# First attention: normalising and rounding on ScalarE, a ninth summand that centres the sums, one bias product for two v tiles

## Chip, cores, metric

One core of a Trainium2 chip (trn2). The metric is the device time of one execution in microseconds (us); of several runs the median is taken.

## The reference

Two blocks of attention and mixture of experts over 4 x 1024 tokens of 256 numbers, all in float32. The change touches only the first attention, which has no softmax: every token mixes its own heads.

```python
xn = _layernorm(x)
q = (xn @ Wq.T + bq)      # 16 heads of 16;  k, v: 8 heads of 16, each used by two heads of q
q = q * cos + _rotate_half(q) * sin          # k the same
def _softmax_kernel(x, R):                   # R: 8 x 16
    n = jnp.sqrt(jnp.sum(x * x, axis=-1, keepdims=True))
    x = x / jnp.maximum(n, 1e-06)
    p = jnp.einsum('...d,ed->...e', x, R)
    return jnp.concatenate([jnp.sin(p), jnp.cos(p)], axis=-1) / math.sqrt(F)
kv = jnp.einsum('bhsf,bhsd->bsfd', kp, v)    # sum over heads, position by position
out = jnp.einsum('bhsf,bsfd->bhsd', qp, kv)
g = _silu(_L0_ffn_ref(xn, L0_ffn_wg, ...))   # 8 experts, the two best of each token
x = x + (out @ Wo.T + bo) * g
```

The product of a q head's features with a k head's is a sum of cosines of eight angle differences. The kernel computes it as the sum of sin^2(pi * d) over the eight differences d (in turns), less 4, with the factor -2 folded into other constants. The second block (causal attention, 16 experts, a shared expert) follows.

## The kernel before

The kernel runs phase by phase with a barrier between. The first is `first_attention`. It goes over 32 tiles of 128 tokens in software-pipelined steps. `in_steps(eng, (lag, stage), ...)` writes each engine's program: in step n it calls every stage with tile n - lag, in the order of its list, after `beside(n)`, which holds work with a pace of its own in the first 24 steps (`BESIDE`). Within an engine the order is that of the program; between engines semaphores connect them. A tile passes through these stages (engine, lag):

- Ahead of the steps ScalarE makes the high half of the weights (`w_all[0]`). A product in float32 is made as three passes of high and low halves (`three_passes`, whose matmuls all stand under L121).
- `statistics` (VectorE, `beside`, four tiles in each of steps 0 to 7) gives mean and variance, `root` (ScalarE, at the start of `beside` of the same step) the square root, `inverse_root` (VectorE, one step later) its inverse. `normalise` (VectorE, L519) writes a pair of normalised tiles to `rows`, one pair in step 1 and two in each step after.
- `transpose` (TensorE) transposes one pair a step, `high_half` (ScalarE) copies it out of PSUM, `low_half` (VectorE, one step later) writes the rest.
- `project` (TensorE, 2): q and k of one tile, seven matmuls, the last with the bias: two rows of ones by `b_two`, which holds the high and low half of all biases. `values_and_logits`: v and the routing logits of a pair, at the end of the step, seven matmuls for each tile, each with its own bias matmul (L778).
- `take_qkv` (ScalarE, 2) copies q and k out (`qk`) and writes their squares (`sq`); `rotate` (GpSimd, 2) makes the rotary step; `square_norm` (VectorE, 3, L530) sums the squares; `transpose_rotated` (TensorE, 3), `keep_rotT` (ScalarE, 3), `random_projection` (TensorE, 4), `keep_p` (ScalarE, 4).
- `norm` (ScalarE, 4), `bounded_norm` and `inverse_norm` (VectorE, 5) work on four tiles at a time, in every fourth step. The root and the sine need different ScalarE tables, so each such step has two table loads.
- `in_turns` (VectorE, 8, L551) gives p divided by the norm and by 2 pi; `whole_turns` (L556) rounds it by adding and subtracting a large constant `ROUND`; `fraction` (L562) is the difference. `differences` (VectorE, 9, L570) writes all q minus k angles to `apart` (16 x 8 x 8 per token), `sines` and `squares` (ScalarE, 10), `sine_sums` (VectorE, 11, L576) sums eight of them to `A`, `centre` (L580) subtracts 4, `weigh` (VectorE, 11, L589) multiplies with v, 2048 numbers per token: the large product.
- `sum_groups` (TensorE, 12, L803) sums the eight groups in PSUM, `take_out` (ScalarE, 13), `store` (SyncE, 14).

In steps 18 to 23 VectorE also does the routing of the experts, which needs all logits. From its step 24 on GpSimd scatters the normalised rows to the experts' slots by indirect DMA, beside the rotations. VectorE's step before is, in this order:

```python
in_steps(dve, (5, bounded_norm), (11, sine_sums), (5, inverse_norm), (8, in_turns), (11, centre), (8, whole_turns), (11, weigh),
         (8, fraction), (3, square_norm), (9, differences), first=BESIDE, beside=beside)
```

## Time and profile before

| | |
|---|---|
| Median of 3 runs | 1822.14 us (1820.26 to 1829.56) |
| Profiled execution | 1824.24 us, span 1822.5 us |
| TensorE, VectorE, ScalarE, GpSimd busy | 1599.4, 1377.4, 1031.1, 669.7 us |
| First attention | the first 322 us of the span |

An execution's own time is a little above the span, which runs from the first to the last recorded instruction. Busy times count overlapping instructions once. An engine that is busy need not be the bound: a VectorE instruction also counts as busy while something outside the program's waits holds it up.

### The profile page before, as it was taken

Reading aid. Unit: us, or ns where it says so; the run is one execution under the profiler, and the core shown is the slowest. Engines: PE = TensorE matmul, PEld = TensorE weight load, DVE = VectorE, ACT = ScalarE, POOL = GpSimd, SP = SyncE. Lnnn points to the kernel's source line nnn. Section 1 sums busy time; section 2 is a strip of 40 time slices with the busy share of each in tenths; the row PEclk is TensorE's granted clock in tenths of the full one; section 3 lists DMA queues with packets and bytes.
Section 4 is the critical chain, followed back from the end, with each engine's and each line's share of the span. In section 5 each row is a group of like instructions: output and inputs, shape, how many; then the busy total and the mean of one; then the engine's idle time right before and its main releaser. Section 6 shows DMA issues by size and latency. Waiting matters only on the chain. (4 is left out here: it accounts for less than half of the span.)

```text
span 1822.5 us, 34561 instructions
## 1 busy us (share of the span) xinstructions
PE 1599.4 (88%) x9650; PEld 1239.4 (68%) x9650; DVE 1377.4 (76%) x3710; ACT 1031.1 (57%) x2457; POOL 669.7 (37%) x842
## 2 busy tenths in 40 slices
PE   5997887889936777999999999987899999998896
PEld 4885666689934564554555555544799999877775
DVE  6899999366667869999888888823666666667777
ACT  2664564356646750665676767674566666543443
POOL 2655688400047613212247676610000000066662
PEclk8998899989976995999999999998999999999998
DMA  9433457744436885322436454424864444355552
GB/s 345 131 87 95 105 133 174 247 132 133 131 114 195 289 318 133 68 64 70 108 95 176 139 165 151 131 58 147 270 190 134 134 132 133 113 171 162 173 165 74
DMA packets 279591, 272.72 MB, mean 150 GB/s; under 512 B 121769, under 2 KB 248426, under 8 KB 277356
## 3 DMA queue, kind: packets, MB, share of 16 engines
q1 hardware_dynamic: 255672, 215.41, 40.2%
q0 software_dynamic: 18432, 50.36, 9.1%
q10 hardware_dynamic: 5332, 4.96, 0.8%
q8 instruction: 88, 1.44, 0.3%
q14 instruction: 67, 0.55, 0.1%
HBM read 136.84 MB, written 133.69 MB: 148 GB/s over the span
## 5 line engine op out<-in xcount | busy, mean ns | idle before, releaser
L1940 ACT ACTIVATE ca_PT<-ca_psS 128x512 f32<-128x512 f32 (+3 forms) x768 | 336.4, 494 | 203.5 <-PE ca_psS L1977 198.6
L1480 POOL DMA_INDIRECT g_y<-ys_scratch,pos x128 | 125.1, 977 | 427.1 <-POOLq L73 356.0
L1856 DVE CUSTOM_DVE_ANT_0 ca_masked_row<-ca_psM,mask_row 128x384 f32<-128x384 f32 (+3 forms) x512 | 224.2, 486 | 44.8 <-PE ca_psM L1960 42.8
L1977 PE MATMUL ca_psS<-ca_QS,ca_KS 128*128 128x512 f32 (+1 forms) x480 | 175.3, 369 | 1.4 <-ACT ca_PT L1940 1.4
L1860 DVE TENSOR_REDUCE ca_part<-ca_psM 128x1 f32<-128x512 f32 x256 | 163.5, 684 | 16.9 <-PE ca_psM L1960 15.6
L1989 PE MATMUL ca_psO<-ca_PT,ca_VA 128*17 128x512 f32 (+3 forms) x1536 | 161.6, 493 | 6.1 <-ACT ca_OT L1932 6.1
L1960 PE MATMUL ca_psM<-ca_KS,ca_QS 126*128 126x512 f32 (+2 forms) x480 | 159.8, 381 | 5.0 <-DVE ca_part L1856 3.8
L803 PE MATMUL fa_psO<-fa_weighed,ident 128*128 128x256 f32 x512 | 130.9, 414 | 37.0 <-DVE fa_weighed L589 36.9
L1977 PEld LDWEIGHTS ca_psS<-ca_QS,ca_KS 128*128 128x128 f32 x480 | 90.6, 190 | 87.6 <-ACT ca_PT L1940 58.5
L391 POOL DMA_INDIRECT xs_scratch<-x_sb,pos x128 | 124.6, 973 | 55.9 <-ACT ca_PT L1940 34.2
L803 PEld LDWEIGHTS fa_psO<-fa_weighed,ident 128*128 128x128 f32 x512 | 103.9, 208 | 58.5 <-DVE fa_weighed L589 43.2
L1032 PE MATMUL f_psU<-ffn_lo,f_x_hi 128*128 x428 | 138.5, 324 | 0.0
L1132 DVE TENSOR_TENSOR f_x_lo<-f_psT,f_x_hi 128x256 fp32r<-128x256 f32 x214 | 90.7, 424 | 49.9 <-ACT f_x_hi L1073 49.7
L1079 ACT ACTIVATE f_silu<-f_psU 128x176 f32<-128x176 f32 x214 | 67.9, 318 | 100.0 <-PE f_psU L1032 99.9
L1831 POOL TENSOR_TENSOR ca_waited<-ca_waited 1x1 f32<-1x1 f32 x128 | 25.6, 200 | 259.3 <-ACT ca_PT L1940 258.0
L1053 PE MATMUL f_psY<-ffn_lo,f_h_hi 128*128 x428 | 120.4, 281 | 0.0
L1960 PE MATMUL ca_psM<-spare 126*128 126x512 f32 (+3 forms) x288 | 98.8, 408 | 16.5 <-DMA ca_VA<-v_scratch 15.9
L1960 PEld LDWEIGHTS ca_psM<-ca_KS,ca_QS 126*128 126x128 f32 x480 | 89.5, 198 | 33.7 <-DVE ca_part L1856 16.5
L1140 DVE TENSOR_TENSOR f_h<-f_silu,f_psU 128x96 f32<-128x96 f32 x214 | 54.2, 253 | 76.8 <-ACT f_silu L1079 76.6
L1977 PE MATMUL ca_psS<-spare 128*128 128x512 f32 (+3 forms) x288 | 104.3, 376 | 2.7 <-ACT ca_PT L1940 2.6
L1032 PE MATMUL f_psU<-ffn_hi,f_x_hi 128*128 x286 | 104.2, 364 | 0.0
L1053 PE MATMUL f_psY<-ffn_hi,f_h_hi 128*128 x286 | 92.4, 323 | 0.3 <-DVE f_h_hi L1149 0.3
(271 smaller groups left out, 4620.6 us busy)
## 6 DMA issues: line engine op xcount, KB each, us to landing
xs_scratch<-fa_blank SPq DMA_DIRECT2D x32, 640.0 KB, 4.9
x_sb<-xs_scratch SPq DMA_DIRECT2D x143, 128.0 KB, 2.1
ys_scratch<-x_sb SPq DMA_DIRECT2D x143, 128.0 KB, 1.7
xs_scratch<-fa_blank SPq DMA_DIRECT2D x32, 384.0 KB, 6.6
spare<-qk_scratch SPq DMA_DIRECT2D x24, 512.0 KB
ca_QS<-qk_scratch SPq DMA_DIRECT2D x20, 512.0 KB
ca_KS<-qk_scratch SPq DMA_DIRECT2D x20, 512.0 KB
x_sb<-in_ffn SPq DMA_DIRECT2D x16, 608.0 KB, 4.1
```

Of the source, the lines that this page charges most:

```text
L391: pool.indirect_dma_start(xs_dram, bass.IndirectOffsetOnAxis(pos[:, t, k:k + 1], 0), rows[:, t, :], None).then_inc(sent[i], 16)
L803: ins = pe.matmul(psO[i % 2][:, 0:NQ], ident[:], weighed[:, i % 2, g, :], start=g == 0, stop=g == KV_HEADS - 1)
L1032: ins = pe.matmul(psU[i % 2][:, 0:WU], x[:, i % 2, k * P:(k + 1) * P], w[:, bass.ds(e, 1), k * WU:(k + 1) * WU].rearrange("p a n -> p (a n)"),
L1053: ins = pe.matmul(psY[i % 2][:, 0:HID], x, w[:, bass.ds(e, 1), first:first + HID].rearrange("p a n -> p (a n)"), start=start, stop=first = ...
L1132: dve.tensor_tensor(x_lo[:, i % 2, :], psT[i % 2][:, 0:HID], x_hi[:, i % 2, :].bitcast(F32), ALU.subtract)\
L1480: pool.indirect_dma_start(y[:, t % R, k, :], None, y_dram, bass.IndirectOffsetOnAxis(pos[:, t, k:k + 1], 0)).then_inc(got[t % R], 16)
L1856: ins = dve.tensor_tensor_reduce(masked_row[:, (n * NU + u) % BANKS, h * w:(h + 1) * w], bank[:, h * w:(h + 1) * w], mask_row[:, CHUNK - w ...
L1860: dve.tensor_reduce(part[:, k0 // CHUNK, h0:h0 + nh, qt], bank[:, 0:nh * w].rearrange("p (h k) -> p h k", h=nh), AX.X, ALU.max).then_inc(u ...
L1940: act.activation(PT[:, s % PTS, h, off:CHUNK], psS[(GH * s + h) % BANKS][:, off:CHUNK], ACT.Exp)\
L1960: ins = pe.matmul(bank[:, h * w:(h + 1) * w], QS[slot][0:STACK, h0 + h, qt * P:(qt + 1) * P], KS[slot][0:STACK, h0 + h, k0:k0 + w], start= ...
L1977: pe.matmul(psS[tile % BANKS][:, off:CHUNK], KS[slot][:, h, kt * P:(kt + 1) * P], QS[slot][:, h, c * CHUNK + off:(c + 1) * CHUNK], start=T ...
L1989: ins = pe.matmul(psO[STRIP * h:STRIP * h + VW, off:CHUNK], VA[:, slot, kt, VW * h:VW * (h + 1)], PT[:, s % PTS, h, off:CHUNK], start=kt = ...
```

## The change

- **Normalising** moves from VectorE to ScalarE: `rows = x * rstd + shift`, with `shift = -mean * rstd` from one more VectorE instruction for each group of four tiles. Pairs 0 and 1 are normalised in step 1, pair n in step n.
- **The root of the variance** moves from the start of ScalarE's step to its end (`after`). A root of one number is put ahead of everything else on ScalarE, so that its table is loaded first.
- **Rounding** (`whole_turns`) moves to ScalarE, between the copy of q and k and their square (`take_qkv` is split in two). `fraction` takes the second half of the rounding along: (whole - ROUND) - turns, which turns the sign of all angles. It now stands behind `square_norm`.
- **Centring**: `apart` gets a ninth column that GpSimd sets to -4 once, the sums read all nine, and `centre` is gone. Differences, sines and squares touch the first eight.
- **Biases of v**: one matmul of 272 columns for both tiles, ahead of their products, in place of one for each tile.
- **Order**: `norm` is the first stage of ScalarE's step. On VectorE the low half of the weights is made ahead of the biases, and `low_half(0)` moves into step 1 between them. `project` waits for the biases only ahead of its first bias matmul.

```diff
@@ first_attention, VectorE
             def inverse_root(g):
-                dve.reciprocal(some, some).then_inc(rstd_done, 1)
-
-            def normalise(q):
-                dve.wait_ge(rstd_done, q * PAIR // GROUP + 1)
-                for t in range(PAIR * q, PAIR * (q + 1)):
-                    dve.tensor_scalar(rows[:, t, :], x_sb[:, t, :], mean_rstd[:, t, 0:1], mean_rstd[:, t, 1:2], ALU.subtract, ALU.mult)\
-                       .then_inc(xn_done, 1)
+                dve.reciprocal(some, some).then_inc(rstd_part, 1)
+                dve.wait_ge(rstd_part, g + 1)
+                dve.scalar_tensor_tensor(shift[:, GROUP * g:GROUP * (g + 1)], mean_rstd[:, GROUP * g:GROUP * (g + 1), 0], -1.0, some,
+                                         ALU.mult, ALU.mult).then_inc(rstd_done, 1)
...
-            def whole_turns(t, i, b):
-                dve.wait_ge(turns_part, t * 2 + 1)
-                dve.tensor_scalar(whole[:, i % 2, :, :], turns[:, i % 2, :, :], ROUND, ROUND, ALU.add, ALU.subtract)\
-                   .then_inc(turns_part, 1)
             def fraction(t, i, b):
-                dve.wait_ge(turns_part, t * 2 + 2)
+                dve.wait_ge(whole_done, t + 1)
                 f = turns[:, i % 2, :, :]
-                dve.tensor_tensor(f, f, whole[:, i % 2, :, :], ALU.subtract).then_inc(turns_done, 1)
+                dve.scalar_tensor_tensor(f, whole[:, i % 2, :, :], ROUND, f, ALU.subtract, ALU.subtract).then_inc(turns_done, 1)
...
-                dve.tensor_tensor(apart[:, i % 2, :, :, :], q4, k4, ALU.subtract).then_inc(apart_done, 1)
+                dve.tensor_tensor(apart[:, i % 2, :, :, 0:RF], q4, k4, ALU.subtract).then_inc(apart_done, 1)
...
-            def centre(t, i, b):
-                dve.wait_ge(A_done, t + 1)
-                dve.tensor_scalar(A[:, i % 2, :, :], A[:, i % 2, :, :], RF / 2.0, None, ALU.subtract).then_inc(centred, 1)
...
-            in_steps(dve, (5, bounded_norm), (11, sine_sums), (5, inverse_norm), (8, in_turns), (11, centre), (8, whole_turns), (11, weigh),
-                     (8, fraction), (3, square_norm), (9, differences), first=BESIDE, beside=beside)
+            in_steps(dve, (5, bounded_norm), (11, sine_sums), (5, inverse_norm), (8, in_turns), (11, weigh), (3, square_norm),
+                     (8, fraction), (9, differences), first=BESIDE, beside=beside)
@@ ScalarE
+            def normalise(q):
+                act.wait_ge(rstd_done, q * PAIR // GROUP + 1)
+                for t in range(PAIR * q, PAIR * (q + 1)):
+                    act.activation(rows[:, t, :], x_sb[:, t, :], ACT.Identity, scale=mean_rstd[:, t, 1:2], bias=shift[:, t:t + 1])\
+                       .then_inc(xn_done, 1)
...
+            def whole_turns(t, i, b):
+                act.wait_ge(turns_part, t + 1)
+                act.activation(whole[:, i % 2, :, :], turns[:, i % 2, :, :], ACT.Copy, bias=ROUND).then_inc(whole_done, 1)
...
             def beside(n):
-                if n < QUADS:
-                    root(n)
+                if n == 1:
+                    normalise(0)
+                    normalise(1)
                 if 0 <= n - 1 < PAIRS:
                     high_half(n - 1)
+                if 2 <= n < PAIRS:
+                    normalise(n)
...
+            def after(n):
+                if n < QUADS:
+                    root(n)
...
-            in_steps(act, (2, take_qkv), (10, sines), (3, keep_rotT), (13, take_out), (10, squares), (4, keep_p),
-                     (4, norm), first=BESIDE, beside=beside)
+            in_steps(act, (4, norm), (2, take_qk), (8, whole_turns), (2, square_qk), (10, sines), (3, keep_rotT), (13, take_out),
+                     (10, squares), (4, keep_p), first=BESIDE, beside=beside, after=after)
@@ TensorE, values_and_logits
+                pe.matmul(psV[:, 0:PAIR * NVE].rearrange("p (t n) -> p t n", n=NVE), ones[:],
+                          b_two[:, NQK:W0].unsqueeze(1).broadcast_to([2, PAIR, NVE]), start=True, stop=False, skip_group_check=True)
                 for j, t in enumerate(range(PAIR * q, PAIR * (q + 1))):
-                    ins = pe.matmul(out, ones[:], b_two[:, NQK:W0], start=False, stop=True, skip_group_check=True)
```

VectorE, a step from the sums on, before (the fa_ names are the first attention's tiles; fa_n are the squared norms, fa_A the sums):

```order
L576 TENSOR_REDUCE fa_A<-fa_apart 128x128
L551 SCALAR_TENSOR_TENSOR fa_turns<-fa_p_sb,fa_inv 128x192
L580 TENSOR_SCALAR fa_A<-fa_A 128x128
L556 TENSOR_SCALAR fa_whole<-fa_turns 128x192
L589 TENSOR_TENSOR fa_weighed<-fa_A,fa_v 128x2048
L562 TENSOR_TENSOR fa_turns<-fa_turns,fa_whole 128x192
L530 TENSOR_REDUCE fa_n<-fa_sq 128x24
L570 TENSOR_TENSOR fa_apart<-fa_turns 128x1024
```

The same stretch with the change:

```order
L573 TENSOR_REDUCE fa_A<-fa_apart 128x128
L553 SCALAR_TENSOR_TENSOR fa_turns<-fa_p_sb,fa_inv 128x192
L582 TENSOR_TENSOR fa_weighed<-fa_A,fa_v 128x2048
L532 TENSOR_REDUCE fa_n<-fa_sq 128x24
L559 SCALAR_TENSOR_TENSOR fa_turns<-fa_whole,fa_turns 128x192
L567 TENSOR_TENSOR fa_apart<-fa_turns 128x128x8
```

Centring and rounding are gone, and the norm's sum stands between the large product and the fraction.

ScalarE, the start of the program, before (spare and wqkvr_raw are the weights and the transposed rows, mean_rstd the statistics, s the normalised rows):

```order
L706 ACT_TABLE_LOAD
L706 ACTIVATE spare<-wqkvr_raw 128x1040
L630 ACT_TABLE_LOAD
L630 ACTIVATE mean_rstd<-mean_rstd 128x4 x2
L636 ACTIVATE spare<-fa_psT 128x512
L630 ACTIVATE mean_rstd<-mean_rstd 128x4
L636 ACTIVATE spare<-fa_psT 128x512
```

And with the change:

```order
L716 ACT_TABLE_LOAD
L716 ACTIVATE fa_warm<-fa_ones 2x1
L718 ACTIVATE spare<-wqkvr_raw 128x1040
L620 ACTIVATE mean_rstd<-mean_rstd 128x4
L625 ACTIVATE s<-x_sb,fa_shift,mean_rstd 128x256 x4
L632 ACTIVATE spare<-fa_psT 128x512
L620 ACTIVATE mean_rstd<-mean_rstd 128x4
L632 ACTIVATE spare<-fa_psT 128x512
```

The second table load is gone, four normalisations stand ahead of the first copy out of PSUM, and the second root, which stood ahead of that copy, stands behind it.

ScalarE, a step with the norms' root, before (the first two rows still belong to the step ahead):

```order
L672 ACT_TABLE_LOAD
L672 ACTIVATE fa_inv<-fa_n 128x96
L636 ACTIVATE spare<-fa_psT 128x512
L642 ACTIVATE fa_v<-fa_psV 128x256
L643 ACTIVATE logits<-fa_psV 128x2x8
L649 ACTIVATE fa_qk<-fa_psQ 128x384
L652 ACTIVATE fa_sq<-fa_psQ 128x384
L677 ACT_TABLE_LOAD
L677 ACTIVATE fa_apart<-fa_apart 128x1024
```

And with the change:

```order
L675 ACT_TABLE_LOAD
L675 ACTIVATE fa_inv<-fa_n 128x96
L645 ACTIVATE fa_qk<-fa_psQ 128x384
L649 ACTIVATE fa_whole<-fa_turns 128x192
L655 ACTIVATE fa_sq<-fa_psQ 128x384
L680 ACT_TABLE_LOAD
L680 ACTIVATE fa_apart<-fa_apart 128x128x8
L661 ACTIVATE fa_rotT<-fa_psR 128x384
```

The root and its load stand ahead of the copy of q and k, and the rounding stands between that copy and the square.

## Rows read from the trace of the kernel before

**Rows 1.** Windows: stretch, length, busy PE, PEld, DVE, ACT, POOL, PEclk, DMA, GB/s.
```profile
0.00:322.00 322.00, 261.90 (x1316) 218.40 (x1316) 293.23 (x459) 165.74 (x309) 196.75 (x186) 0.93 0.54 153
```

**Rows 2.** Windows, two stretches of 20 us.
```profile
100.00:120.00 20.00, 20.00 (x116) 17.40 (x116) 19.91 (x24) 13.81 (x26) 12.90 (x12) 1.00 0.32 79
240.00:260.00 20.00, 17.78 (x92) 14.98 (x92) 19.91 (x25) 13.65 (x23) 18.26 (x17) 1.00 0.51 141
```

**Rows 3.** Timeline, first 20 us, ScalarE and TensorE: start, length, engine, line, tiles [idle before].
```profile
7.72 1.28 ACT L630 ACT_TABLE_LOAD   x1
...
18.37 1.11 PE L757 MATMUL fa_psT<-ident,s 128*128 128x128 f32 x4 [6.94 <-DVE s L519]
19.14 0.67 PE L121 MATMUL fa_psQ<-spare 128*128 128x384 f32 x1
```

**Rows 4.** Timeline from 28 to 75 us, ScalarE and TensorE.
```profile
28.37 0.21 ACT L630 ACTIVATE mean_rstd<-mean_rstd 128x4 f32<-128x4 f32 x1 [5.58 <-DVE mean_rstd L509]
...
29.55 0.45 PE L121 MATMUL fa_psV<-spare 128*128 128x136 f32 x1 [3.10 <-ACT logits L643]
...
34.06 0.67 PE L121 MATMUL fa_psQ<-spare 128*128 128x384 f32 x1
...
74.76 0.42 PE L121 MATMUL fa_psQ<-spare 128*128 128x384 f32 x1
```

**Rows 5.** Windows, granted clock (PEclk) and matmuls (x) of TensorE.
```profile
30.00:44.00 14.00, 14.00 (x54) 12.23 (x54) 9.65 (x30) 3.83 (x12) 6.31 (x8) 0.50 1.07 371
59.00:76.00 17.00, 17.00 (x114) 14.53 (x113) 12.73 (x24) 10.42 (x24) 11.52 (x14) 1.00 0.25 83
```

**Rows 6.** Timeline of TensorE, one step from its v products on.
```profile
96.31 0.27 PE L121 MATMUL fa_psV<-spare 128*128 128x136 f32 x1
...
96.77 0.33 PE L121 MATMUL fa_psV<-spare 128*128 128x136 f32 x1
...
98.26 0.42 PE L121 MATMUL fa_psQ<-spare 128*128 128x384 f32 x1
...
106.82 0.42 PE L121 MATMUL fa_psQ<-spare 128*128 128x384 f32 x1
```

**Rows 7.** Timeline of VectorE, parts of two steps.
```profile
195.45 1.15 DVE L562 TENSOR_TENSOR fa_turns<-fa_turns,fa_whole 128x192 f32<-128x192 f32 x1
196.52 0.54 DVE L530 TENSOR_REDUCE fa_n<-fa_sq 128x24 f32<-128x384 f32 x1
...
200.86 0.22 DVE L580 TENSOR_SCALAR fa_A<-fa_A 128x128 f32<-128x128 f32 x1
200.99 0.25 DVE L556 TENSOR_SCALAR fa_whole<-fa_turns 128x192 f32<-128x192 f32 x1
201.16 2.29 DVE L589 TENSOR_TENSOR fa_weighed<-fa_A,fa_v 128x2048 f32<-128x2048 f32 x1
203.36 0.35 DVE L562 TENSOR_TENSOR fa_turns<-fa_turns,fa_whole 128x192 f32<-128x192 f32 x1
```

**Rows 8.** Groups of instructions to 340 us: count, busy time, mean ns, idle before.
```profile
L570 DVE TENSOR_TENSOR fa_apart<-fa_turns 128x1024 f32<-128x1024 f32 x32 | 43.0, 1344 | 0.0
...
L576 DVE TENSOR_REDUCE fa_A<-fa_apart 128x128 f32<-128x1024 f32 x32 | 38.6, 1207 | 4.0 <-ACT fa_apart L682 3.9
...
L677 ACT ACTIVATE fa_apart<-fa_apart 128x1024 f32<-128x1024 f32 x32 | 33.9, 1059 | 30.4 <-DVE fa_apart L570 30.3
...
L562 DVE TENSOR_TENSOR fa_turns<-fa_turns,fa_whole 128x192 f32<-128x192 f32 x32 | 20.6, 643 | 0.1
...
L688 ACT ACTIVATE fa_out<-fa_psO 128x256 f32<-128x256 f32 x32 | 12.1, 377 | 8.2 <-PE fa_psO L803 8.2
...
L556 DVE TENSOR_SCALAR fa_whole<-fa_turns 128x192 f32<-128x192 f32 x32 | 11.4, 357 | 0.1
...
L580 DVE TENSOR_SCALAR fa_A<-fa_A 128x128 f32<-128x128 f32 x32 | 10.6, 330 | 0.1
```

**Rows 9.** The routing's additions: shortest, median and longest ns.
```profile
L310 DVE TENSOR_TENSOR r_cum<-r_cum x10: 291/414/1046, 157.6 to 806.3; 128x128 f32<-128x128 f32 x5, 128x256 f32<-128x256 f32 x5
```

More of the change, by code:

```diff
@@ L170, in _, with in_steps @@
                 dve.wait_ge(lo_done, len(pairs))
-def in_steps(eng, *stages, tiles=TILES, first=None, beside=None):
+def in_steps(eng, *stages, tiles=TILES, first=None, beside=None, after=None):
     most = max(lag for lag, _ in stages)
@@ L189, in in_steps @@
         step(n)
+        if after is not None:
+            after(n)
     with eng.Fori(first // POS_TILES, whole) as b:
@@ L590, in weigh, with split_weights_and_bias @@
                    .then_inc(weighed_done, 1)
+            def split_weights_and_bias():
+                dve.wait_ge(whi_done, 1)
+                dve.tensor_tensor(w_all[1], w_raw[:], w_all[0].bitcast(F32), ALU.subtract).then_inc(wlo_done, 1)
+                dve.wait_ge(ident_in, 16)
+                dve.wait_ge(bias_in, 16)
+                s = Steps(dve, bias_part)
+                s.link(dve.tensor_copy(b_hi[:, :], bias[:, :]))
+                s.link(dve.tensor_tensor(b_lo[:, :], bias[:, :], b_hi[:, :].bitcast(F32), ALU.subtract))
+                low_half(0)
+                s.link(dve.tensor_scalar(b_lo[:, :], b_lo[:, :], ident[0:2, 1:2], None, ALU.mult))
+                s.link(dve.scalar_tensor_tensor(b_two[:, :], b_hi[:, :].bitcast(F32), ident[0:2, 0:1], b_lo[:, :], ALU.mult, ALU.add))
             def beside(n):
-                if 0 <= n - 2 < PAIRS:
+                if 1 <= n - 2 < PAIRS:
                     low_half(n - 2)
@@ L596, in beside @@
                     inverse_root(n - 1)
-                for q in normalised(n):
-                    normalise(q)
                 if n == 1:
-                    split_bias_and_weights()
+                    split_weights_and_bias()
                 if n < QUADS:
@@ L607, in beside @@
                     route(at)
-            def normalised(n):
-                return [q for q in (2 * n - 3, 2 * n - 2) if 0 <= q < PAIRS]
-            def split_bias_and_weights():
-                dve.wait_ge(ident_in, 16)
-                dve.wait_ge(bias_in, 16)
-                s = Steps(dve, bias_part)
-                s.link(dve.tensor_copy(b_hi[:, :], bias[:, :]))
-                s.link(dve.tensor_tensor(b_lo[:, :], bias[:, :], b_hi[:, :].bitcast(F32), ALU.subtract))
-                s.link(dve.tensor_scalar(b_lo[:, :], b_lo[:, :], ident[0:2, 1:2], None, ALU.mult))
-                s.link(dve.scalar_tensor_tensor(b_two[:, :], b_hi[:, :].bitcast(F32), ident[0:2, 0:1], b_lo[:, :], ALU.mult, ALU.add))
-                dve.wait_ge(whi_done, 1)
-                dve.tensor_tensor(w_all[1], w_raw[:], w_all[0].bitcast(F32), ALU.subtract).then_inc(wlo_done, 1)
-            in_steps(dve, (5, bounded_norm), (11, sine_sums), (5, inverse_norm), (8, in_turns), (11, centre), (8, whole_turns), (11, weigh),
-                     (8, fraction), (3, square_norm), (9, differences), first=BESIDE, beside=beside)
+            dve.wait_ge(ones_done, 3)
+            in_steps(dve, (5, bounded_norm), (11, sine_sums), (5, inverse_norm), (8, in_turns), (11, weigh), (3, square_norm),
+                     (8, fraction), (9, differences), first=BESIDE, beside=beside)
         @block.scalar
@@ L674, in sines @@
             def sines(t, i, b):
-                s = apart[:, i % 2, :, :, :]
+                s = apart[:, i % 2, :, :, 0:RF]
                 act.wait_ge(apart_done, t + 1)
@@ L730, in _ @@
             pool.memset(blank[:, :], 0.0).then_inc(ones_done, 1)
+            pool.memset(apart[:, :, :, :, RF:RF + 1], -RF / 2.0).then_inc(ones_done, 1)
             routing.ranks(pool)
```

30 lines of the change are left out of this document (18 added, 12 removed).

## Prediction

> **What bounds the kernel now.** I read the windows first, then the timeline of the first attention, because the diff touches nothing else. That phase is 322 us of the span, and VectorE is busy for 293 of them [rows 1]. Windows of 20 us show two regimes in it [rows 2]. From 100 to 120 us TensorE is busy without a gap (20.00), and VectorE nearly so (19.91); one step's q/k product starts at 98.26 and the next one's at 106.82 [rows 6], so a step takes 8.56 us. From 240 to 260 us VectorE is still full (19.91), TensorE is not (17.78), ScalarE has 6.35 us free, and GpSimd is busy for 18.26: there VectorE sets the pace. The timeline of the first 80 us adds a third regime. TensorE waits 6.94 us for the second pair of rows to be normalised, and the first q/k product starts only at 19.14 [rows 3]. Then ScalarE waits 5.58 us for VectorE's statistics, with its copies queued behind that root; TensorE sits idle for 3.10 us until the logits are copied, and the third tile's product starts at 34.06 [rows 4]. From 30 to 44 us TensorE has a granted clock of 0.50, its lower level (1.2 GHz), although it has no gap; later, at 1.00, it does 114 matmuls in 17 us instead of 54 in 14 [rows 5]. A step there has 34 of them (7 for q/k, 14 for v, 4 and 3 transposes, 6 projections), so 5.1 us at full clock. Step 11's product starts at 74.76 [rows 4].
>
> **Start.** (1) The root's table is loaded ahead of the copy of the weights, so the 1.28 us load at 7.72 [rows 3] is off the chain. (2) ScalarE normalises both first pairs in step 1. TensorE's second transposes stand ahead of its first product and waited for statistics till 18.37; now four normalised tiles are ready at about 10.5. The first pair is then transposed and split (the weights' low half and two short bias steps stand ahead of its low half on VectorE), and the first product starts at about 12, 7 us sooner. (3) TensorE's step 2 has 25 matmuls: at 0.26 us each, as at the low clock [rows 5], 6.5 us. Step 3 has 28: at 0.15, 4.2. That gives 22.7 for the third tile's product. I add 1.8 for the copy of the first tile and its rotation, which the transposes of step 3 wait for: 24.5 instead of 34.06, 9.6 us gained. (4) From there to step 11 it took 40.7 us for seven steps, part of it at the low clock. Now ScalarE's root stands behind its copies, so the statistics hold up no copy, and VectorE is rid of four normalisations a step. TensorE should be the bound at 5.1 less 0.28 (next part), with waits of a microsecond at most and no fall of the clock: 33.8 us, 6.9 gained. Step 11 comes at 58.3 instead of 74.8: 16.5 us.
>
> **TensorE.** Between the last product of one v tile and the first of the next, with the bias product between, lie 0.46 us [rows 6]. Of two such bias products a step one stays, with twice the columns and still with its own weights to load. The gain is between nothing and 0.46; I take 0.28. In steps 12 to 17, where TensorE is the bound, five steps give 1.4 us.
>
> **VectorE from step 18 on.** Each of the last 26 steps loses the centring and the rounding: start to start 0.13 and 0.17 us [rows 7]. The sums read nine summands now, an eighth of 1207 ns more [rows 8]: 0.15. Net 0.15 a step, 3.9 us. The fraction takes 0.35 us where nothing is in its way, 1.15 where something is [rows 7], 643 ns in the mean [rows 8]: some 37% of its instructions wait 0.8 us. It stood right behind the large product. Now the norm's sum stands between, 0.54 long [rows 7] and 0.46 from start to start, and uses that much of the wait: ten of the 26 steps, 4.4 us. Together 8.3.
>
> The mean durations would say more: centring 330, rounding 357 [rows 8], and the fraction's whole 0.3, less 0.15, make 0.8 a step, 22 us. I take the low reading: the tails in those means are turns of GpSimd, and without centring and rounding the large product behind them meets the same turn. The Trainium skill (SBUF — State Buffer, "Who interferes with whom") says that VectorE and GpSimd share one port pair under an exclusive lock, that whoever issues second is blocked until the first ends, and that a reduction never takes it. By that rule the 0.8 us is the rest of a GpSimd instruction, the norm's sum hides 0.46 of it, and this term is 8.3; without it, by the means, 22. The trace agrees in that the sums, a reduction, have no tail (mean 1207).
>
> **What is added, and its cover.** ScalarE gets 32 normalisations and 32 roundings, each at most like a 128x256 copy, 377 ns [rows 8]: 24 us, into its free time. The rounding waits for VectorE's turns of the same step; behind it stand the square of q/k, the sines (1059 ns [rows 8]) and the squares, and VectorE's sums wait for these one step later. Rounding, square, sines, two copies and squares are about 3.3 us; VectorE has large product (2.2 [rows 7]), norm's sum, fraction and differences (1.2 at least [rows 8]) in that time, 4.1. One step in four has two table loads of 1.28 more on ScalarE, one of them now ahead of the rounding; there the cover is gone and up to 0.5 us can show. In steps 10 and 11 loads, normalisations and first sines meet while TensorE's step is only 4.8: I subtract 1.4 us. The root at the front of the step costs nothing, since the norm's sum that it needs ends in VectorE's step before. GpSimd's extra memset lies before the first rows land.
>
> **Sum.** 16.5 + 1.4 + 8.3 - 1.4 = 24.8 us of the profiled execution's 1824.24: 1799.4. The median of the runs is 2.1 lower, 1797.3; I say 1798. What follows is the same code behind a barrier and only shifts.
>
> **Rivals.** (a) *TensorE falls to its low clock in the start all the same.* In 30 to 44 us it did 54 matmuls instead of 94, 6 us lost; with the waits that bring it about 7 less are gained: 1805. For it: it stayed low through 14 us without a gap. Against: the fall came behind an idle stretch of 3.10 us, and I expect none so long. (b) *ScalarE becomes what is waited for.* In steps 4 to 12 its copies get two normalisations and a rounding more, 1.1 us, within TensorE's 4.8, and in every step its wait for the turns delays all behind it. If 0.5 us shows in 14 steps up to 17 and 0.3 in the 26 others, 15 us go: 1813. The Trainium skill (ScalarE: Activation LUTs, "Rules for kernel authors" and "What ACT_TABLE_LOAD costs") speaks against this change: adds and multiplies belong on VectorE, and each pointer operand adds about 93 ns. By its figures a normalisation takes 0.59 us (estimate); no row here shows one. Against (b): ScalarE is free for a third of the later steps [rows 2]. (c) *More is gained*: VectorE's part comes nearer to the means, 7 us more: 1791. (d) *Slower.* Differences and sums walk over nine elements per group where they walked over eight. The slowest of the routing's additions, some of which skip elements too, took 1046 ns, the fastest 291 [rows 9]. If those 0.75 us are the skipping's and not a turn of GpSimd's, differences and sums pay 1.5 us in each of 26 steps, 39 less the gain of 25: 1836. It decides from 0.95 us a step on. Against: the blocked fraction, whose operands are dense, carries the same 0.8. (e) *Nothing moves*: the start's gain is waited away before step 18 by something the trace hides under TensorE's pace, and only VectorE's 8 us or less remain: 1816.
>
> **Numbers.** Forecast 0.50 (1790 to 1803), (a) 0.18, (b) 0.14, (c) 0.09, (d) 0.04, (e) 0.05. A range without (d), (e), and the outer parts of (b) and (c) is 1788 to 1812. About 0.5% (9 us) can be told from no change here. Faster takes the forecast, (a), (b) and (c): 0.91; same (e), 0.05; slower (d), 0.04.
>
> **What would show it.** First product near 12 us, third near 24.5, step 11's near 58; granted clock 1.00 from about 20 us on; steps of 8.3 us in TensorE's regime; the fraction's mean near 480 ns, with no wait for ScalarE's rounding; sums of 1.35 us; a phase 25 us shorter and nothing changed behind it. I am wrong if differences take over 1.6 or sums over 1.5 us, if VectorE waits over 10 us before its sums, or if the granted clock is 0.50 between 20 and 60 us.

## The result, and the profile after

The changed kernel takes 1808.12 us (median of 8 runs, 1805.35 to 1812.45); the kernel before, run beside it on the same chip, 1821.32 us (8 runs, 1818.79 to 1829.56). The ratio is 0.9929 with a 95% interval of [0.9916, 0.9943]: 13.2 us faster. The forecast was 1798, a gain of 24.8 us; the direction was right and half of the size was missing. The profiled execution took 1808.26 us, its span 1806.5, which is 16.0 less than the span before.

The windows of the changed kernel from its first instruction to the end of the first attention, which answer to [rows 1] (the phase now ends near 306 us instead of 322), and the stretches between large products on VectorE (first, second, 5th, 6th, 7th, 8th, 14th, 25th and 32nd). PEclk is the granted clock of TensorE.

```profile
core 0: us, PE busy (x) PEld busy (x) DVE busy (x) ACT busy (x) POOL busy (x), PEclk, DMA share, GB/s
0.00:306.00 306.00, 255.99 (x1300) 215.83 (x1300) 279.15 (x371) 186.41 (x373) 202.12 (x187) 0.93 0.56 160
...
61.40:70.60 9.20, 7.63 (x36) 6.81 (x37) 8.29 (x11) 9.11 (x19) 4.24 (x4) 0.81 0.20 67
...
124.80:182.50 57.70, 44.17 (x182) 36.50 (x183) 55.15 (x86) 30.99 (x55) 21.88 (x23) 0.80 0.35 84
182.50:263.00 80.50, 70.57 (x343) 59.79 (x342) 80.32 (x71) 49.99 (x93) 73.86 (x56) 0.92 0.51 133
263.00:298.20 35.20, 26.51 (x112) 21.11 (x111) 34.72 (x33) 19.19 (x29) 28.80 (x22) 0.95 0.77 193
```

The same stretches of the kernel before:

```profile
78.50:87.20 8.70, 7.50 (x44) 6.43 (x44) 8.61 (x12) 8.55 (x15) 7.71 (x7) 1.00 0.01 2
...
142.20:201.20 59.00, 43.46 (x185) 35.69 (x186) 57.05 (x98) 27.99 (x46) 29.39 (x23) 0.83 0.30 75
201.20:278.50 77.30, 67.83 (x332) 56.22 (x332) 77.12 (x93) 45.18 (x79) 66.06 (x55) 0.96 0.56 144
278.50:314.40 35.90, 26.24 (x110) 20.96 (x109) 35.62 (x43) 17.91 (x24) 29.50 (x22) 0.95 0.71 176
```

The reader is to lay the stretches side by side. The first large product starts at 61.4 instead of 78.5 us, 17.1 sooner. From there to the 8th it is 63.4 us instead of 63.8; to the 14th 57.6 instead of 58.9; to the 25th 80.5 instead of 77.3; to the 32nd 35.2 instead of 35.9. The lead is 17.1, 17.4, 18.7, 15.5 and 16.2 us. So the start is the whole gain of the phase. The 24 steps from the 8th to the 32nd, to which nearly all of the prediction's 8.3 us belong, took 172.2 us and now take 173.4. VectorE has no gap in the stretch of 80.5 us (80.32 busy) with 71 instructions instead of 93: they became longer.

The start on TensorE's timeline, which answers to [rows 3, 4], and two windows of the same kernel. In the names, fa_psQ is the q/k product, fa_psV the value product, fa_psT the transposes of the normalised rows:

```profile
10.62 1.11 PE L770 MATMUL fa_psT<-ident,s 128*128 128x128 f32 x4
12.39 0.66 PE L121 MATMUL fa_psQ<-spare 128*128 128x384 f32 x1 [0.66 <-DVE spare L527]
...
18.77 0.67 PE L121 MATMUL fa_psQ<-spare 128*128 128x384 f32 x1
...
23.00 0.28 PE L121 MATMUL fa_psV<-wqkvr_lo,spare 128*128 128x136 f32 x1
23.11 0.39 PE L121 MATMUL fa_psV<-spare 128*128 128x136 f32 x2
23.33 0.28 PE L121 MATMUL fa_psV<-wqkvr_lo,spare 128*128 128x136 f32 x1
...
24.27 0.42 PE L121 MATMUL fa_psQ<-spare 128*128 128x384 f32 x1
```

```profile
30.00:40.00 10.00, 10.00 (x69) 8.47 (x68) 9.59 (x28) 7.43 (x22) 6.36 (x9) 1.00 1.09 382
60.00:64.00 4.00, 3.26 (x21) 2.93 (x21) 4.00 (x4) 3.97 (x11) 0.09 (x1) 0.85 0.80 272
64.00:68.00 4.00, 3.31 (x15) 2.81 (x14) 3.37 (x5) 3.97 (x6) 3.92 (x4) 0.72 0.00 0
```

First product 12.39 (said: about 12), third 24.27 (said 24.5), then one every 4.77 us at a granted clock of 1.00, and step 11's at 58.51 (said 58.3). Only behind it does the clock fall: to its lower level, 0.50, from 63 to 66 us (0.72 is the mean of 64 to 68), after TensorE had stood idle for 0.74 us at 62.0. Between the second and the 5th large product the steps took 6.94 us each, much less than the 8.3 said for TensorE's regime, and the step behind them 12.2 instead of 8.7.

The groups of VectorE between the 14th and the 25th large product, before and then after (count | busy us, mean ns of one | idle time before):

```profile
L589 DVE TENSOR_TENSOR fa_weighed<-fa_A,fa_v 128x2048 f32<-128x2048 f32 x12 | 27.4, 2280 | 0.0
L570 DVE TENSOR_TENSOR fa_apart<-fa_turns 128x1024 f32<-128x1024 f32 x11 | 16.9, 1538 | 0.0
...
L562 DVE TENSOR_TENSOR fa_turns<-fa_turns,fa_whole 128x192 f32<-128x192 f32 x11 | 7.0, 636 | 0.0
L551 DVE SCALAR_TENSOR_TENSOR fa_turns<-fa_p_sb,fa_inv 128x192 f32<-128x192 f32 x11 | 6.1, 551 | 0.2
```

```profile
L582 DVE TENSOR_TENSOR fa_weighed<-fa_A,fa_v 128x2048 f32<-128x2048 f32 x12 | 31.8, 2649 | 0.0
L567 DVE TENSOR_TENSOR fa_apart<-fa_turns 128x1024 f32<-128x1024 f32 x11 | 16.4, 1488 | 0.0
L573 DVE TENSOR_REDUCE fa_A<-fa_apart 128x128 f32<-128x1152 f32 x11 | 14.7, 1340 | 0.0
L553 DVE SCALAR_TENSOR_TENSOR fa_turns<-fa_p_sb,fa_inv 128x192 f32<-128x192 f32 x12 | 9.0, 748 | 0.3
L559 DVE SCALAR_TENSOR_TENSOR fa_turns<-fa_whole,fa_turns 128x192 f32<-128x192 f32 x11 | 8.2, 741 | 0.0
```

The large product went from 2280 to 2649 ns and the turns from 551 to 748, though neither instruction was edited; the fraction (L562, then L559), said to fall to a mean near 480 ns, went from 636 to 741 here and from 643 only to 620 over the whole phase; the sums cost the forecast eighth (1340 ns; 1207 in [rows 8]).

What follows the first attention, from the next phase's first transposes to the end of the span, is 1495.3 us before (1822.5 less 327.16) and 1495.1 after (1806.5 less 311.42). In the traces of all the kernels below it lies between 1489.4 and 1497.7 with no order in it. A span alone therefore tells no difference of a few us here; below, distances inside the phase are compared, and medians where a kernel was timed.

### The profile page after: what moved, and what is told of

It is laid out like the page before. It is cut to its first block and busy times, and to the rows that moved or that the text cites. A ratio compares the mean times of both kernels' runs of the same rounds, so it can differ in the third digit from the quotient of the medians.

```text
span 1806.5 us, 34538 instructions
## 1 busy us (share of the span) xinstructions
PE 1591.2 (88%) x9634; PEld 1233.5 (68%) x9634; DVE 1365.1 (76%) x3622; ACT 1052.4 (58%) x2521; POOL 675.2 (37%) x843
## 5 line engine op out<-in xcount | busy, mean ns | idle before, releaser
L1874 DVE TENSOR_REDUCE ca_part<-ca_psM 128x1 f32<-128x512 f32 x256 | 163.6, 685 | 16.5 <-PE ca_psM L1974 15.1
L818 PE MATMUL fa_psO<-fa_weighed,ident 128*128 128x256 f32 x512 | 127.0, 405 | 8.7 <-DVE fa_weighed L582 6.7
L1093 ACT ACTIVATE f_silu<-f_psU 128x176 f32<-128x176 f32 x214 | 68.1, 318 | 101.2 <-PE f_psU L1046 101.2
L1974 PEld LDWEIGHTS ca_psM<-ca_KS,ca_QS 126*128 126x128 f32 x480 | 88.7, 196 | 35.9 <-DVE ca_part L1870 17.3
```

Of the source, the lines that this page charges most:

```text
L818: ins = pe.matmul(psO[i % 2][:, 0:NQ], ident[:], weighed[:, i % 2, g, :], start=g == 0, stop=g == KV_HEADS - 1)
L1874: dve.tensor_reduce(part[:, k0 // CHUNK, h0:h0 + nh, qt], bank[:, 0:nh * w].rearrange("p (h k) -> p h k", h=nh), AX.X, ALU.max).then_inc(u ...
L1974: ins = pe.matmul(bank[:, h * w:(h + 1) * w], QS[slot][0:STACK, h0 + h, qt * P:(qt + 1) * P], KS[slot][0:STACK, h0 + h, k0:k0 + w], start= ...
```

## Experiments

Three theories stood at first. **A**: VectorE's short instructions were long because GpSimd's instructions hold both up, and that time is conserved: take one instruction away and the next one meets it. **B**: ScalarE's rounding, which waits for VectorE's turns, gives back what VectorE gains. **C**: nine summands at a stride cost more than an eighth.

The distance from the 8th to the 32nd large product, 24 steps, is called D: 172.2 us before, 173.4 after. Two executions of one kernel (the late changed one below) differ by 0.8 us in it.

**Start and joint bias product alone.** VectorE's and ScalarE's steps are those of before:

```diff
-            in_steps(dve, ..., (8, in_turns), (11, weigh), (3, square_norm),
-                     (8, fraction), (9, differences), ...)
+            in_steps(dve, ..., (8, in_turns), (11, centre), (8, whole_turns), (11, weigh),
+                     (8, fraction), (3, square_norm), (9, differences), ...)
```

> The start, the roots and the joint bias as changed; VectorE's centring, rounding, fraction right behind the large product, the norms' root last in ScalarE's step as before. Theory A (GpSimd's turns on VectorE are conserved, so taking two short instructions off VectorE gives nothing while GpSimd is as loaded): first large product at 61 us as in the changed kernel, distance from the 14th to the 23rd large product 66 us as in both, ratio to before within 0.003 of the changed kernel's 0.993. Rival B (ScalarE's new wait for the turns eats an 8 us gain): the distance stays at 66 us here too, since here nothing is saved, but from the first to the eighth large product it falls below 63 us, because the stalls on fraction and sums there are gone. Rival C (the ninth summand and the stride of nine cost): 3 to 5 us faster than the changed kernel.

Measured: 1810.51 us (7 runs, 1804.94 to 1814.9), ratio 0.9942 [0.9921, 0.9964]; first large product at 61.6, D 172.9. The interval overlaps that of the changed kernel, and the first large product is 0.2 us from its own. The start holds the gain, and the change of the steps adds nothing that can be measured. From the first to the 8th large product it takes 64.2 us, where B said less than 63. The step of TensorE's regime is 8.2 us here, as the prediction said.

**Centring back on VectorE, eight dense summands.**

```diff
-        apart = sb("apart", [P, 2, HEADS, KV_HEADS, RF + 1])
+        apart = sb("apart", [P, 2, HEADS, KV_HEADS, RF])
+            def centre(t, i, b):
+                dve.wait_ge(A_done, t + 1)
+                dve.tensor_scalar(A[:, i % 2, :, :], A[:, i % 2, :, :], RF / 2.0, None, ALU.subtract).then_inc(centred, 1)
```

> As the changed kernel, but sums over eight dense values and centring on VectorE again. A: no difference, within 2 us of the changed kernel (1808), the waits of the large product falling by what centring takes up. C: 3 us faster if the ninth summand costs more than the centring. By my prediction's reading: 0.13 less 0.15 a step, nothing.

Measured: 1809.4 us, ratio 0.9940 [0.9918, 0.9963]; D 177.4, 4.1 more than the changed kernel. Its centring takes 0.42 us from start to start, 0.29 more than the 0.13 that the prediction read in [rows 7]; it is never under 0.25 there, with the large product right behind it, where the rounding stood between.

**Rounding back on VectorE**, with the ninth summand:

```diff
+            def whole_turns(t, i, b):
+                dve.wait_ge(turns_part, t * 2 + 1)
+                dve.tensor_scalar(whole[:, i % 2, :, :], turns[:, i % 2, :, :], ROUND, ROUND, ALU.add, ALU.subtract)\
+                   .then_inc(turns_part, 1)
```

> As the changed kernel, but rounding on VectorE again, between turns and large product. A: within 2 us of the changed kernel. B: faster than the changed kernel by 3 us or more, the gain lying between the first and the eighth large product (63 us there in the changed kernel, with 4.9 us idle) and at the places where rotations now come late. By my prediction: 5 us slower (0.17 a step in 26 steps).

Measured: 1810.12 us, ratio 0.9935 [0.9911, 0.9959]; D 175.4, 2.0 more.

**The fraction ahead of the norm's sum**, right behind the large product:

```diff
-            in_steps(dve, ..., (11, weigh), (3, square_norm), (8, fraction), (9, differences), ...)
+            in_steps(dve, ..., (11, weigh), (8, fraction), (3, square_norm), (9, differences), ...)
```

> As the changed kernel, but the fraction right behind the large product and the norm's sum behind it. By my prediction: 4 us slower, the fraction's mean up by some 150 ns. A: within 2 us, the fraction's wait up and the differences' wait down by as much. B says nothing of it, except that the fraction may wait for ScalarE's rounding more often.

Measured: 1809.93 us, ratio 0.9932 [0.9909, 0.9954]; D 176.5, 3.1 more. Each of the three parts, undone alone, lengthens D by 2.0 to 4.1; undone together (the first run) they shorten it by 0.4. The parts do not add up, which points to where GpSimd's instructions fall in the step. B does not explain it: from 60 to 300 us VectorE waits for the rounding for 4.9 us in this trace, 2.4 in the one with the centring back, 2.3 in the changed kernel, and all these waits lie ahead of the 8th large product, outside D. A fits the medians, which agree within their intervals, but not D: it had said no difference.

The traces show which instruction pays. The large product takes 2.20 us from start to start where nothing is in its way. Over D the 24 of them take 0.1 us more than that in the kernel before, 0.9 with the start alone and 1.3 with the rounding back: in these three the rounding stands right before the product. They take 5.3 more in the changed kernel, 4.1 with the fraction first and 7.4 with the centring back, where no rounding stands before the product. So the rounding, and not the centring, keeps the large product clear; what it saves there is paid elsewhere, since D is no shorter with it.

**GpSimd quiet, in the kernel before and in the changed one.** Both leave out most of the rotation of q and k (16 of 384 columns are rotated, the rest is a constant) and start the scatters late:

```diff
-        PREFIXED, SENT = 21, BESIDE
+        PREFIXED, SENT = 21, TILES + 2
-                q3, a3, b3 = (x.rearrange("p (h d) -> p h d", d=D) for x in (qk[:, i % 2, :], rot_a[:, :], rot_b[:, :]))
+                q3, a3, b3 = (x.rearrange("p (h d) -> p h d", d=D)[:, 0:1, :] for x in (qk[:, i % 2, :], rot_a[:, :], rot_b[:, :]))
```

> The kernel before, with GpSimd quiet in the first attention: it rotates 16 of a tile's 384 columns (the rest of each rotated tile is a constant, so most of the rotation is left out), and its scatters start only once all tiles are rotated. Measured by the distance between large products on VectorE. Theory A (what VectorE's short instructions lose is GpSimd's turn of memory access, and it is conserved): no tails are left, turns 0.3 us, fraction 0.35, rounding 0.3, centring 0.26, large product 2.2; a step of about 5.8 us from the 14th to the 23rd large product instead of 7.3. Theory B (ScalarE's new wait eats the gain) says nothing of this run, it is the reference of the next.

> The changed kernel made quiet in the same way (most of the rotation left out, scatters late). Theory A: with nothing of GpSimd's to wait for, the step is shorter than in the quiet kernel before by what the instructions themselves take, 0.13 + 0.17 - 0.15 = 0.15 us, so nine steps from the 14th to the 23rd large product are about 1.4 us shorter, and VectorE does not wait for ScalarE's rounding. Theory B: VectorE waits for the rounding or the squares, and the nine steps are equal or longer. Theory C (nine summands at a stride are slower than an eighth more): sums over 1.35 us or differences over 1.3 us without any load on GpSimd.

One step of each on VectorE's timeline, the kernel before first (start, length):

```profile
192.50 2.28 DVE L589 TENSOR_TENSOR fa_weighed<-fa_A,fa_v 128x2048 f32<-128x2048 f32 x1
194.71 0.35 DVE L562 TENSOR_TENSOR fa_turns<-fa_turns,fa_whole 128x192 f32<-128x192 f32 x1
...
197.70 0.35 DVE L551 SCALAR_TENSOR_TENSOR fa_turns<-fa_p_sb,fa_inv 128x192 f32<-128x192 f32 x1
197.96 0.22 DVE L580 TENSOR_SCALAR fa_A<-fa_A 128x128 f32<-128x128 f32 x1
198.10 0.26 DVE L556 TENSOR_SCALAR fa_whole<-fa_turns 128x192 f32<-128x192 f32 x1
198.26 2.29 DVE L589 TENSOR_TENSOR fa_weighed<-fa_A,fa_v 128x2048 f32<-128x2048 f32 x1
```

```profile
184.15 2.29 DVE L582 TENSOR_TENSOR fa_weighed<-fa_A,fa_v 128x2048 f32<-128x2048 f32 x1
...
186.81 0.35 DVE L559 SCALAR_TENSOR_TENSOR fa_turns<-fa_whole,fa_turns 128x192 f32<-128x192 f32 x1
187.08 1.22 DVE L567 TENSOR_TENSOR fa_apart<-fa_turns 128x1024 f32<-128x1024 f32 x1
188.21 1.35 DVE L573 TENSOR_REDUCE fa_A<-fa_apart 128x128 f32<-128x1152 f32 x1
...
189.74 2.29 DVE L582 TENSOR_TENSOR fa_weighed<-fa_A,fa_v 128x2048 f32<-128x2048 f32 x1
...
194.60 1.35 DVE L573 TENSOR_REDUCE fa_A<-fa_apart 128x128 f32<-128x1152 f32 x1 [0.59 <-ACT fa_apart L685]
```

Every tail is gone. The step is 5.76 us before and 5.59 after: 0.17 less, for a forecast of 0.15. The differences, whose result now lies at a stride of nine, take 1.22 us here as in the quiet kernel before, so theory C is out. But in one step of four VectorE waits for ScalarE's squares (0.59 above), and the nine steps from the 14th to the 23rd large product came out only 0.3 us shorter (53.6 for 53.9), not 1.4. D is 152.5 and 150.8 us: the steps' change is worth 1.7 us with GpSimd quiet, and GpSimd costs the kernel before 19.7 us (172.2 less 152.5) and the changed one 22.5. So B has a part, by way of the squares and not of the rounding. Within D VectorE waits 2.1 us for the squares and not at all for the rounding (6.7 and 3.2 us of such waits lie ahead of it), and the quiet kernel before has no such wait in D: with GpSimd out of the way that takes half of what the shorter instructions would give (24 times 0.17, 4.1 us).

**Scatters late, rotations whole**, in both kernels (the first line of the diff above alone):

> The kernel before with its scatters started only once all tiles are rotated, rotation whole. It splits GpSimd's load in two: the rotations are left, the scatters are gone from the stretch. If the scatters' descriptors take turns from VectorE as the rotations do, the nine steps from the 14th to the 23rd large product shrink by up to what 15 scatters in 80 us (1.38 us each) take, some 1 us a step; if only the rotations do, they stay at 65.8 us.

> The changed kernel with its scatters late in the same way. Theory A: the nine steps are as long as those of the late kernel before, within 1 us, since GpSimd's rotations are the same in both and wait on either one instruction or its neighbour; the difference to the run before with scatters on time says how much of the changed kernel's long instructions (4.30 us for one large product) is scatters.

From the 14th to the 23rd large product: 63.6 us in the late kernel before (65.8 with the scatters) and 61.7 in the late changed one (66.5). They are 1.9 apart, where A as I had written it said equal within 1. D is 170.1 and 165.7: the scatters cost the kernel before 2.1 us and the changed one 7.7. With them out of the way, the steps' change is worth 4.4 us. Less the quiet kernels' D, the rotations cost 17.6 us before and 14.9 with the change, so what GpSimd costs is not conserved: it fell by 2.7 for the rotations and rose by 5.6 for the scatters (2.0 and 4.8 by the second execution below). The one execution of the late kernel before took 1822.2 us, no less than the kernel before; that of the late changed kernel took 1800.46, and that led to the next pair.

**The late changed kernel and the late kernel with the start alone, timed.**

> The changed kernel with its scatters started only once all tiles are rotated, timed; one execution gave 1800.46. Theory A2 (the scatters, 1.0 to 2.9 us each on GpSimd between two rotations, are what the changed step loses to): its gain of 8 us over the changed kernel is real, median 1800 to 1803, ratio 0.989 to 0.990, faster than both kernels by their intervals. If that execution was a stray one, the median is 1806 to 1810.

> Start and joint bias of the changed kernel, VectorE's and ScalarE's steps as before (rounding and centring on VectorE), scatters late. Theory A2: with the scatters out of the way the changed step is worth what the traces of the two late kernels differ by behind the start (3.7 us from the 8th to the 25th large product), so this kernel is 3 to 4 us slower than the run before: last large product at 294, median 1804 to 1806. If the changed step is worth nothing with late scatters either, both medians are equal within 1 us. If it is worth what the prediction said (8.3), this one comes at 1808 or above.

Measured: 1810.48 us (6 runs, 1803.23 to 1815.41), ratio 0.9948 [0.9928, 0.9968], and 1809.0 us (5 runs), ratio 0.9946 [0.9931, 0.9961]; D 166.5 and 170.3, again 3.8 apart. Both medians are those of the changed kernel within the intervals, so the version that one execution made look 8 us better is not better. Two rows say where the phase's gain goes. The first transposes of the next phase, in the changed kernel and then in the late one:

```profile
311.42 3.14 PE L1016 MATMUL f_psT<-ident,room 128*128 128x128 f32 x10 [7.17 <-DMA room<-o_scratch]
```

```profile
314.22 1.12 PE L1016 MATMUL f_psT<-ident,room 128*128 128x128 f32 x4 [13.21 <-DMA room<-o_scratch]
```

The wait for the attention's output to come back from memory is 13.2 us instead of 7.2: 6.0 of the 6.9 that D lost are given back there. The late scatters stand in that stretch. In all six traces with late scatters this wait is 10.4 to 13.2 us, in all eight with the scatters on time 6.6 to 7.2. So starting the scatters late lengthens it; how they delay the transfer was not shown.

The other part is in the start. TensorE in the third step, the changed kernel above (value products 0.11 us apart at 23.00 to 23.33) and this one:

```profile
23.59 0.41 PE L121 MATMUL fa_psV<-wqkvr_lo,spare 128*128 128x136 f32 x1
23.80 0.63 PE L121 MATMUL fa_psV<-spare 128*128 128x136 f32 x2
...
26.01 0.67 PE L121 MATMUL fa_psQ<-spare 128*128 128x384 f32 x1
```

The same products are 0.21 us apart, and the next q/k product starts at 26.01 instead of 24.27, the one after it at 32.2 instead of 29.1. The windows give both a granted clock of 1.00. The first large product came at 64.5 here and at 64.8 in the run with the fraction first, at 61.0 in an earlier execution of this same kernel: an execution may or may not lose 3.5 us there (two of the nine traces that have this start in full do).

**Normalisation back on VectorE**, all else changed:

```diff
+            def normalise(q):
+                dve.wait_ge(rstd_done, q * PAIR // GROUP + 1)
+                for t in range(PAIR * q, PAIR * (q + 1)):
+                    dve.tensor_scalar(rows[:, t, :], x_sb[:, t, :], mean_rstd[:, t, 0:1], mean_rstd[:, t, 1:2], ALU.subtract, ALU.mult)\
+                       .then_inc(xn_done, 1)
```

> The changed kernel with the normalisations on VectorE at their old place, everything else as changed. It prices part 2 and 4 of the start: if moving them is what starts the products early, the first q/k product comes at 17 to 18 us, TensorE falls to its low clock again between 20 and 50 us, and the first large product is 8 to 14 us later than 61.4. If the warm table and the order of ScalarE's step did it, the first product is at 13 to 14 and the first large product at 62 to 64.

Measured: 1812.88 us, one execution. First product at 17.7, third at 27.1, step 11's at 65.6, first large product at 68.1 (61.4 in the changed kernel). The clock, in windows of this kernel:

```profile
28.00:36.00 8.00, 7.88 (x55) 6.56 (x54) 7.83 (x22) 4.71 (x16) 4.18 (x5) 1.00 1.09 384
36.00:44.00 8.00, 7.17 (x42) 6.42 (x42) 7.76 (x23) 2.41 (x9) 5.50 (x8) 0.80 1.05 360
44.00:60.00 16.00, 16.00 (x102) 13.75 (x101) 15.04 (x40) 8.50 (x26) 9.00 (x12) 0.89 1.02 341
```

Moving the normalisations is worth 6.7 of the start's 17.1 us in this one execution, less than the 8 to 14 said. The first product came as said. The clock fell as said: the 0.80 and 0.89 are means of windows in which the granted clock was 0.50 from 42 to 44 us and 0.54 from 44 to 48. That is its lower level again, for some 6 us, where the kernel before spent about 17 us there (28 to 45) and the changed one none up to 60 us. The longest idle stretch of TensorE from its first product to that fall is 0.81 us, right ahead of it (to 40.5). The other 10.4 us are left for the table loaded early, the root behind the copies and the joint product; the first two were not taken apart.

**Two bias products as before**, all else changed:

```diff
-                pe.matmul(psV[:, 0:PAIR * NVE].rearrange("p (t n) -> p t n", n=NVE), ones[:],
-                          b_two[:, NQK:W0].unsqueeze(1).broadcast_to([2, PAIR, NVE]), start=True, stop=False, skip_group_check=True)
+                    ins = pe.matmul(out, ones[:], b_two[:, NQK:W0], start=False, stop=True, skip_group_check=True)
```

> The changed kernel with two bias products per pair of value tiles as before. The prediction's term is 0.28 us a step while TensorE is the bound: q/k products 5.05 us apart in steps 4 to 10 instead of 4.77, first large product 1.9 us later (63.3), large products 7.2 apart from the 2nd to the 5th instead of 6.94. If the joint product brings nothing, they stay at 4.77 and 6.94, and the first large product at 61.4.

Measured: 1809.51 us, one execution. The q/k products of steps 4 to 10 are 5.09 us apart instead of 4.77: 0.32 a step, where 0.28 was said. The first large product is at 64.8, 3.4 later (1.9 said). The third q/k product is already 1.5 us late (25.76 for 24.27), behind two steps in which products ran at the wider spacing of the paragraph above; how much of that the second bias product makes was not taken apart. The rest comes from the steps behind it, at 0.32 each. From the first to the 8th large product it takes 65.0 us instead of 63.4, though the large products 2 to 5 stay 6.97 apart (7.2 said): this is VectorE's own pace there (20.8 of 20.8 us busy in the changed kernel, TensorE 20.3), and the longer TensorE step shows from the 6th on.

## Why the prediction was half right

**As a whole.** The forecast was 24.8 us and 1790 to 1803 us; measured were 13.2 us and 1808. That this lies inside the range of 1788 to 1812 is luck: the range reaches there only by the rivals (a) and (b), and neither is what happened. The start's term came as said, and VectorE's term of 8.3 us, the greater part of what is missing, came out below nothing.

**Start, 16.5 us: right.** 17.1 at the first large product, 16.2 at step 11's product. Its chain held at each of the four places that it named, in the profiled execution; two of the nine traces with this start come 3.5 us later. The prediction argued that the clock would hold without a gap as long as the 3.10 us in [rows 4]. With the normalisations back the clock fell to 0.50 with no gap over 0.81 us ahead of it, and in the changed kernel at 63 us with one of 0.74, so such a gap is not needed. The late pair gives 15.0 (76.0 less 61.0): the size varies by some us between executions.

**TensorE, 1.4 us: right as a cost, gone in the whole.** Undoing the joint product costs 1.5 us between the first and the 8th large product, in one execution. But the stretch as a whole gained 0.3. Its first step became longer (9.2 us for 8.8) at a mean granted clock of 0.81, where before it was 1.00: the fall that used to come in the start comes behind it.

**VectorE from step 18 on, 8.3 us: this step failed.** The prediction read two sizes off [rows 7]: 0.15 a step net for centring, rounding and ninth summand, and 4.4 us for the norm's sum between large product and fraction. The first is right where GpSimd is quiet (0.17). The second was a sum of waits: "uses that much of the wait: ten of the 26 steps". The run with the fraction first gives it 3.1 us of D, but all the edits together gave -1.2 (or -0.4 against the kernel with the start alone). In its place the runs showed this. The shorter instructions are worth 4.1 us in 24 steps, and waits for the squares take back 2.1 (1.7 us are left, measured with GpSimd quiet). GpSimd's work costs the 24 steps 19.7 us before and 22.5 after, 2.8 more, where the prediction had it cost 4.4 less; 1.7 less 2.8 is the -1.2 measured. The prediction itself said of centring and rounding that the large product behind them meets the same turn, and then did not apply that to the fraction. The fraction's excess over its quiet length fell from 6.3 to 4.7 us (22 of them, start to start), while the large product's rose from 0.0 to 5.3 and the turns' from 3.4 to 4.8 (21 of them). By the rule that the prediction cited (the Trainium skill, "SBUF — State Buffer", "Who interferes with whom") the blocked one waits until the other's instruction ends; the trace agrees in that the sums and the norm's sum have no tail in any run, and in that the other instructions' tails are gone with GpSimd quiet. What the rule does not give is which instruction will pay.

The place where the changed kernel loses more is the scatters: 6.9 to 7.7 us of D for 2.1. Here one falls between two rotations and the large product meets both (GpSimd, then VectorE, changed kernel):

```profile
245.17 1.25 POOL L737 TENSOR_TENSOR fa_rot_b<-fa_qk,sin 128x192 f32<-128x192 f32 x2
...
248.51 1.01 POOL L393 DMA_INDIRECT xs_scratch<-s,pos  x1 [0.15 <-POOL fa_rot L740]
249.55 1.01 POOL L732 TENSOR_TENSOR fa_rot_a<-fa_qk,cos 128x384 f32<-128x384 f32 x1
250.50 3.20 POOL L737 TENSOR_TENSOR fa_rot_b<-fa_qk,sin 128x192 f32<-128x192 f32 x2
```

```profile
248.69 0.34 DVE L553 SCALAR_TENSOR_TENSOR fa_turns<-fa_p_sb,fa_inv 128x192 f32<-128x192 f32 x1
248.96 4.30 DVE L582 TENSOR_TENSOR fa_weighed<-fa_A,fa_v 128x2048 f32<-128x2048 f32 x1
253.18 0.54 DVE L532 TENSOR_REDUCE fa_n<-fa_sq 128x24 f32<-128x384 f32 x1
```

The large product takes 4.30 us instead of 2.28 and GpSimd's two sine products 3.20 together, where a step earlier they took 1.25: both sides lose. It is the only product of such a length, and over D the products are not where the scatters cost: with the scatters late their excess is still 5.7 us (5.3 on time), while the turns give back about 3 us and the differences and the fraction about 2 each. What the rounding's going did is another thing: with it put back the product's excess falls from 5.3 to 1.3. Why the rounding lets GpSimd pass and the centring does not is not shown.

**ScalarE, -1.4 us, and rival (b).** From 60 to 130 us VectorE waits 2.3 us for the rounding, once, and 2.9 for the squares, three times. That is more than the term subtracted, but the kernel before waits 3.9 us for the squares, once, ahead of its first large product (0.9 here), and the 2.3 and the longest wait for the squares fall between the 5th and the 6th large product, where TensorE has no gap (12.20 of 12.20 us). With the rounding back on VectorE that stretch takes 12.0 us instead of 12.2. The waits:

```profile
DVE fa_A L573 <- ACT fa_apart L685: 2.9, 3, 1.1
DVE fa_turns L559 <- ACT fa_whole L649: 2.3, 1, 2.3
```

Rival (b) asked for 0.3 in each of the 26 later steps and did not come. The 32 normalisations took 584 to 606 ns each, not the 377 of [rows 8] that the prediction gave as the most; two in a row take 1.08 us together, since the second starts before the first has ended. The estimate of 0.59 us that the prediction worked out from the Trainium skill ("ScalarE: Activation LUTs", "What ACT_TABLE_LOAD costs") was right. Rivals (a), (d) and (e) did not come either: no clock of 0.50 from 20 to 60 us, differences 1488 ns in the mean, a start that lasts to the end.

**Median and span.** The phase gained 15.7 us by the next phase's transposes, the medians 13.2 with an interval of about 2.5 either side. The start that loses 3.5 us in some executions of the changed kernel fits the difference, but is not shown to be it.

## What to carry to other kernels

Where two engines hold each other up, the time of a short instruction above its undisturbed length belongs to neither: removing or moving the instruction surely saves the undisturbed length only, and the rest may be paid by the next one. So the sum is made with undisturbed lengths, and the contention is entered once, as a term of the whole stretch that may move a few us either way (here -2.7 us for the rotations, +5.6 for the scatters). A chain in the start that nothing overlaps is forecast by walking it instruction by instruction, and that walk held here to 1 us at four places, in six of the nine traces with this start. One execution that looks 8 us better proves nothing about a kernel's time; look where the next phase waits before counting it.

## What the runs showed that I had not expected

- Three parts of an edit whose undoing costs 2.0, 3.1 and 4.1 us of D one at a time are worth -0.4 us together: single undoings don't sum where instructions of two engines interlock.
- The pattern is reproducible all the same. Two executions of the late changed kernel have first large products 3.6 us apart, and the stretch from the 14th to the 25th is 73.6 us in one and 73.5 in the other.
- TensorE's products ran at twice the spacing (0.21 us for 0.11) up to 21 us in one execution and past 28 in another, while the windows give a granted clock of 1.00 throughout. The granted clock alone does not tell that a stretch ran at full speed; the spacing of equal matmuls does.
- A scatter shares GpSimd with the rotations, and moving all scatters out of the phase gave 6.0 of 6.9 us back as a longer wait (13.2 us for 7.2) at the start of the next phase.
